# The FFN tail of a gated expert block: who rounds to the fp8 grid, TensorE or VectorE

## The chip, the core and the metric

The kernel runs on one core of one Trainium2 chip. The metric is the time of one execution on the device in microseconds (us). Names: PE is TensorE (matrix multiply), DVE is VectorE, ACT is ScalarE, POOL is GpSimd, SP is SyncE.

## The reference

The input is 2048 tokens of 512 values. A first part (layer norm, then one of four expert MLPs chosen by the token's id, added back with a gate) is the same before and after. The tail is what matters here:

```python
def _quant_e4m3(t):
    amax = jnp.max(jnp.abs(t)).astype(jnp.float32)
    scale = jnp.maximum(amax / E4M3_MAX, 1e-12)
    fp8 = (t.astype(jnp.float32) / scale).astype(jnp.float8_e4m3fn)
    return (fp8, scale)
...
w_fp8, w_scale = _quant_e4m3(weight)
x_fp8, x_scale = _quant_e4m3(x2d)
out2d = _scaled_mm(x_fp8, w_fp8.T, x_scale, w_scale)   # fp32 product * (sa*sb), then bf16
...
x = x + jnp.tanh(g_ffn[0]) * _L0_ffn_ref(_layernorm(x, axis=-1), L0_ffn_weight)
```

The scale is the maximum over the whole tensor, so nothing of the tail can start before the last token's second layer norm is known. Every value is then rounded to the e4m3 grid (three mantissa bits), multiplied by a 512x512 rounded weight and added to the residual.

## The kernel before

The tokens are sorted by expert into 16 tiles of 128 (a tile is 128 partitions x 512 values). The residual `x1` and the normalised rows `h2` of all tiles lie in SBUF. After the maximum is known (about 153 us into the span) the tail runs over 10 groups of tiles, set by `FIRST` (L168): group 0 is tile 0, group 1 tile 1, groups 2 to 7 are two tiles each (2-3, 4-5, 6-7, 8-9, 10-11, 12-13), group 8 is tile 14 and group 9 tile 15.

Rounding works without an fp8 type. A magic number `vm` is made from the value's size, the scaled value is added to it (`vt`, fp32), and subtracting `vm` again leaves the value rounded to the grid. The subtraction can be done in two places:

- on DVE: `rounded` (L1086) writes `q8 = vt - vm` in bf16, and PE transposes `q8` by multiplying it with the identity (L584, four bf16 products a tile);
- on PE: the transpose itself does it. `vm` is multiplied with the negative identity (L575, four bf16 products) and `vt` with the fp32 identity (L578, four fp32 products) into the same PSUM, so the sum that stands there is `vt - vm`, transposed.

`split(g)` (L259) says which tiles of a group go which way, by `BY_TENSOR` (L170). With 2, the groups 0 to 2 (tiles 0 to 3) are rounded by PE alone. In every later group the first tile is rounded by DVE and, where there is a second one, that one by PE. These are seven tiles on DVE: 4, 6, 8, 10, 12, 14 and 15.

Each engine has its own fixed order, and semaphores join them:

- ACT, in group g's turn: copy the transposed group out of PSUM (`copy_qT`, L727), the scaled absolute value of group g+4 (`scaled`, L721), and the product of group g-1 out of PSUM as bf16 (`to_bf16`, L736, "y" below).
- DVE, in group g's turn: `grid(g+1)` (L1073), `shifted(g)` (L1079), `rounded(g)` (L1086), and `finish(g-3)` (L1090), which adds the gated product to the residual.
- PE: `transposed(g+1)` (L575, L578, L584), then the four products a tile of group g with the rounded weight (L599, "the final products" below). Then the next group.
- POOL: sixteen stores in the order of the tiles (`store_tile`, L365). Each is an indirect DMA that puts a tile's rows back in the tokens' order, and waits until its group is finished.

So a group's way is: transposed, copied, multiplied, "y", finished, stored. Below, store n is the store of tile n.

Of the kernel before, what the change touches and what calls it, by code (L numbers as in the profile page):

```python
# [43 lines left out]
def gated_experts_kernel(nc, x, ids, ctx_t, g_x, g_f, wf_t, out):  # L44
# [10 lines left out]
    with ExitStack() as stack:  # L55
        def sb(name, shape, dt):
            return stack.enter_context(nc.sbuf_tensor(name, shape, dt))
# [109 lines left out]
        qT = sb("qT", [P, NF, D], BF16)  # L167
        FIRST = [0, 1, 2, 4, 6, 8, 10, 12, 14, 15, TILES]  # L168
        GROUPS = len(FIRST) - 1
        BY_TENSOR = 2  # L170
        y8 = sb("y8", [P, NB, D], BF16)

        four_ps = psum("four_ps", [P, 4 * D], F32)
# [82 lines left out]
        def tiles_of(g):  # L256
            return range(FIRST[g], FIRST[g + 1])

        def split(g):  # L259

            tiles = list(tiles_of(g))
            return (tiles[:1], tiles[1:]) if g > BY_TENSOR else ([], tiles)

# [155 lines left out]
        def _(pe):  # L419
# [147 lines left out]
            def transposed(g):  # L567
# [12 lines left out]
                if by_dve:  # L580
                    pe.wait_ge(q8_done, g - BY_TENSOR)
                for i in by_dve:
# [551 lines left out]
```

## Time and profile before

| | before |
|---|---|
| median of 3 runs | 196.71 us (196.63 to 196.82) |
| profiled execution, its own time | 196.66 us |
| its span (first to last instruction) | 194.8 us |
| PE / DVE / ACT / POOL busy, share of the span | 80% / 77% / 57% / 43% |
| start of the last store in the span | 189.05 us |

The tail is the last fifth of the span. Shares over the whole span say little about it, so the rows below are cut by time: start in us from the span's beginning, then duration in us. A row with "x8" stands for eight instructions in a row. The ends of PE's rows are modelled, so where PE runs without a gap, what a piece of work occupies is read from one row's start to the next row's start. Each fp32 product shows as two matmul records.

### The profile page before, as it was taken

What the parts mean: (1) busy time and instruction counts of PE and PEld (TensorE: products, weight loads), DVE (VectorE), ACT (ScalarE), POOL (GpSimd) and SP (SyncE); (2) the same over time, 40 slices, a digit from 0 to 9 for tenths busy, and PEclk for the clock granted to TensorE, in tenths of its full rate; (3) what the DMA queues carried; (4) which work ended last, traced back from release to release, by engine and by line L of the source; (5) the groups of instructions that cost most, each with busy time, mean ns of one, the idle gap of its engine ahead of it and who ended that gap; (6) DMA issues with size and microseconds to landing.
All of it is one profiled execution on the core that took longest, in us unless ns stands there. A gap on an engine that the chain in (4) does not pass through costs nothing.

```text
span 194.8 us, 3253 instructions
## 1 busy us (share of the span) xinstructions
PE 156.2 (80%) x822; PEld 80.3 (41%) x828; DVE 151.0 (77%) x346; ACT 112.0 (57%) x166; POOL 83.0 (43%) x117
## 2 busy tenths in 40 slices
PE   0151969799999799899999899999978799999300
PEld 0110435244555344444444445545433487765000
DVE  2876799898766799899998888677686698999600
ACT  3256698597342855767797644334322698977500
POOL 8258887512311443224456685111102003588770
PEclk9999999999999999999999999999999999999955
DMA  0937998400000221122211211000000001133351
GB/s 3 359 125 191 377 400 273 113 2 0 0 3 0 56 54 30 27 54 57 54 29 40 44 27 27 3 0 0 2 5 0 0 0 57 54 162 162 162 217 54
DMA packets 15440, 15.68 MB, mean 80 GB/s; under 512 B 10816, under 2 KB 11328, under 8 KB 15424
## 3 DMA queue, kind: packets, MB, share of 16 engines
q1 hardware_dynamic: 12576, 7.09, 12.1%
q0 software_dynamic: 2560, 8.39, 12.0%
q8 instruction: 8, 0.13, 0.3%
q14 instruction: 8, 0.07, 0.1%
q10 hardware_dynamic: 288, 0.00, 0.1%
HBM read 8.92 MB, written 4.19 MB: 67 GB/s over the span
## 4 chain that ended last, share of the span: by engine, by line
PE 35%; DVE 29%; issue 14%; POOL 12%; ACT 5%; DMA 1%; DVEq 1%; POOLq 0%
PE four_ps L466 9%; PE four_ps L458 9%; PE four_ps L475 9%; POOL out L365 6%; POOL x L342 3%; DVE zT_lo L899 3%; PE four_ps L504 3%; DVE bn L865 3%; DVE bn L913 2%; DVE w_lo L857 2%; PE q_ps L578 2%; DVE x L907 2%; DVE z L894 1%; DMA ids_s<-in_ids 1%; POOL rstd L352 1%
## 5 line engine op out<-in xcount | busy, mean ns | idle before, releaser
L360 POOL TENSOR_TENSOR rstd<-var,minus_half 128x1 f32<-128x1 f32 x16 | 8.8, 550 | 49.8 <-DVE var L921 49.8
L365 POOL DMA_INDIRECT out<-x,token_of x16 | 20.1, 1255 | 19.9 <-DVE x L1090 15.9
L458 PE MATMUL four_ps<-w_hi,hT_hi 128*128 x76 | 21.4, 393 | 1.4 <-ACT w_hi L626 1.3
L665 ACT ACTIVATE zT_hi<-four_ps 128x512 f16<-128x512 f32 x19 | 11.3, 595 | 18.2 <-PE four_ps L504 18.2
L654 ACT ACTIVATE sg<-four_ps,job_inv_a 128x512 f32<-128x512 f32 x19 | 12.9, 679 | 13.7 <-PE four_ps L475 12.5
L342 POOL DMA_INDIRECT x<-in_x,token_of x16 | 17.4, 1091 | 7.1 <-issue 4.2
L458 PE MATMUL four_ps<-w_hi,zT_hi 128*128 x76 | 19.5, 379 | 1.1 <-DVE x L907 1.1
L645 ACT ACTIVATE w<-x,nmr,rstd 128x512 f32<-128x512 f32 x16 | 13.0, 810 | 12.8 <-DVE nmr L927 12.4
L466 PE MATMUL four_ps<-w_lo,hT_hi 128*128 x76 | 19.7, 381 | 0.0
L475 PE MATMUL four_ps<-w_hi,zT_lo 128*128 x76 | 19.5, 379 | 0.0
L466 PE MATMUL four_ps<-w_lo,zT_hi 128*128 x76 | 19.5, 379 | 0.0
L907 DVE SCALAR_TENSOR_TENSOR x<-four_ps,job_mul,x 128x512 f32 x19 | 14.2, 746 | 6.2 <-PE four_ps L475 6.1
L504 PE MATMUL four_ps<-ident,z 128*128 128x128 f32 x76 | 12.1, 281 | 5.2 <-DVE z L894 4.9
L599 PE MATMUL four_ps<-wf_q,qT 128*128 128x512 bf16 x60 | 15.1, 379 | 0.8 <-ACT qT L727 0.6
L475 PE MATMUL four_ps<-w_hi,hT_lo 128*128 x60 | 15.4, 379 | 0.0
L640 ACT ACTIVATE h<-x,nmr,rstd 128x512 f32<-128x512 f32 x16 | 12.9, 804 | 3.5 <-DVE nmr L881 3.5
L894 DVE SCALAR_TENSOR_TENSOR z<-four_ps,job_z_mul,sg 128x512 f32<-128x512 f32 x16 | 12.0, 749 | 3.4 <-ACT sg L654 3.4
L352 POOL TENSOR_TENSOR rstd<-var,minus_half 128x1 f32<-128x1 f32 x16 | 8.9, 556 | 12.7 <-DVE var L873 12.6
L899 DVE TENSOR_TENSOR zT_lo<-four_ps,zT_hi 128x512 f16<-128x512 f32 x19 | 13.1, 690 | 0.6
L626 ACT ACTIVATE w_hi<-w,w_bits 128x512 f16<-128x512 f32 x16 | 10.2, 711 | 5.8 <-DVE w_bits L810 5.8
L504 PEld LDWEIGHTS four_ps<-ident,z 128*128 128x128 f32 x76 | 8.5, 140 | 11.7 <-DVE z L894 9.1
L857 DVE SCALAR_TENSOR_TENSOR w_lo<-w,w_bits,w_hi 128x512 f16<-128x512 f32 x16 | 11.6, 750 | 1.8 <-ACT w_hi L626 1.7
(146 smaller groups left out, 316.7 us busy)
## 6 DMA issues: line engine op xcount, KB each, us to landing
w<-in_ctx_t SPq DMA_DIRECT2D x4, 1024.0 KB, 9.4
wf<-in_wf_t SPq DMA_DIRECT2D x1, 512.0 KB, 15.1
x<-in_x,token_of POOLq DMA_INDIRECT x16, 5.7
out<-x,token_of POOLq DMA_INDIRECT x16, 2.9
hT_hi<-h_row SPq DMA_TRANSPOSE x9, 2.3
hT_lo<-h_row SPq DMA_TRANSPOSE x9, 2.3
ids_s<-in_ids SPq DMA_DIRECT2D x1, 8.0 KB, 2.9
g_s<-in_g_x ACTq DMA_DIRECT2D x1, 0.5 KB, 2.7
```

The lines of the kernel that those rows point to most:

```text
L342: pool.indirect_dma_start(block_of(x1, i), None, x, bass.IndirectOffsetOnAxis(ap=token_of[:, i:i + 1], axis=0), bounds_check=T - 1).then_i ...
L365: pool.indirect_dma_start(out, bass.IndirectOffsetOnAxis(ap=token_of[:, i:i + 1], axis=0), block_of(x1, i), None, bounds_check=T - 1).then ...
L458: pe.matmul(ps, lhs_hi(k), w_block(w_hi, expert, k), start=(k == 0), stop=False)
L466: mm = pe.matmul(ps, lhs_hi(k), w_block(w_lo, expert, k), start=False, stop=(first is not None and k == K - 1))
L475: mm = pe.matmul(ps, lhs_lo(k), w_block(w_hi, expert, k), start=False, stop=(k == K - 1))
L504: mm = pe.transpose(zT_ps[:, k * P:(k + 1) * P], z[:, k * P:(k + 1) * P], ident[:, :])
L599: mm = pe.matmul(four_ps[:, i % 4 * D:(i % 4 + 1) * D], qT[:, i % NF, k * P:(k + 1) * P], wf_q[:, k * D:(k + 1) * D], start=(k == 0), stop ...
L645: act.activation(block_of(h2, i), block_of(x1, i), ACT.Identity, bias=nmr2[:, :], scale=rstd2[:, :])\
L857: dve.scalar_tensor_tensor(out=w_block(w_lo, e, k), in0=w_block(w32, e, k), scalar=w_scale(e, S_W), in1=w_block(w_hi, e, k), op0=ALU.mult, ...
L894: dve.scalar_tensor_tensor(out=z[:, :], in0=a_ps[:, :], scalar=job_z_mul[:, j:j + 1], in1=sg[:, :], op0=ALU.mult, op1=ALU.mult).then_inc(z ...
L899: dve.tensor_tensor(zT_lo[:, :], zT_ps[:, :], zT_hi[:, :], ALU.subtract).then_inc(zT_lo_done, 1)
L907: dve.scalar_tensor_tensor(out=block_of(x1, tile), in0=y_ps[:, :], scalar=job_mul[:, bass.ds(j, 1)], in1=block_of(x1, tile), op0=ALU.mult, ...
```

## The change

`BY_TENSOR` becomes `GROUPS`, which is 10. No group's number is larger than that, so `split` gives every tile to PE.

```diff
-        BY_TENSOR = 2
+        BY_TENSOR = GROUPS
```

The function that reads it, and what PE does with the answer (the lines are the same before and after):

```python
def split(g):
    tiles = list(tiles_of(g))
    return (tiles[:1], tiles[1:]) if g > BY_TENSOR else ([], tiles)
...
for i in by_pe:      # vm with minus_ident (bf16), vt with ident (fp32)
...
if by_dve:           # q8 with ident_bf
    pe.wait_ge(q8_done, g - BY_TENSOR)
```

On PE, the order of the program in groups 3 to 9 (of each group of two tiles, `q_ps` is the PSUM that takes the transposed tiles, `hT_hi` holds `vm` and `q8`, `w_hi` holds `vt`, `four_ps` takes the final products):

```order
 L575 MATMUL q_ps<-minus_ident,hT_hi 128x128 x4
 L578 MATMUL q_ps<-ident,w_hi 128x128 x4
-L584 MATMUL q_ps<-ident_bf,hT_hi 128x128 x4
+L575 MATMUL q_ps<-minus_ident,hT_hi 128x128 x4
+L578 MATMUL q_ps<-ident,w_hi 128x128 x4
 L599 MATMUL four_ps<-wf_q,qT 128x512 x8
```

In the place of the four bf16 products of the DVE-rounded tile stand four bf16 and four fp32 products. Groups 8 and 9, of one tile each, change in the same way.

On DVE, the turns of groups 5 and 6:

```order
 L1073 TENSOR_SCALAR hT_hi<-hT_lo 128x1024
 L1079 SCALAR_TENSOR_TENSOR w_hi<-w,x_inv,hT_hi 128x1024
-L1086 TENSOR_TENSOR hT_hi<-w_hi,hT_hi 128x512
 L1090 SCALAR_TENSOR_TENSOR x<-y,tg,x 128x1024
 L1073 TENSOR_SCALAR hT_hi<-hT_lo 128x1024
 L1079 SCALAR_TENSOR_TENSOR w_hi<-w,x_inv,hT_hi 128x1024
-L1086 TENSOR_TENSOR hT_hi<-w_hi,hT_hi 128x512
 L1090 SCALAR_TENSOR_TENSOR x<-y,tg,x 128x1024
```

The rounding between `shifted` and `finish` is gone, in all seven groups; nothing else moves on DVE. ACT, POOL and SP have the same instructions in the same order.

## Rows read from the trace of the kernel before

**Rows 1.** Chain of waits, merged, in the tail: start, us, engine, tile, line

```profile
166.44 0.69 DVE hT_hi L1086
167.13 1.24 DVE x L1090
...
169.16 1.57 POOL out L365
```

**Rows 2.** Stretches: busy us of each engine, granted TensorE clock, DMA share, GB/s

```profile
158.90:161.25 2.35, 2.35 (x25) 2.32 (x24) 2.30 (x4) 1.56 (x2) 0.00 (x0) 1.00 0.00 0
162.10:177.90 15.80, 15.64 (x122) 11.00 (x124) 15.01 (x20) 13.48 (x15) 10.40 (x8) 1.00 0.24 100
182.60:190.00 7.40, 0.00 (x0) 0.00 (x0) 1.11 (x2) 0.68 (x1) 5.88 (x6) 0.73 0.44 180
```

**Rows 3.** Timeline of PE: start us, us, line, operation, count, [idle before <-releaser]

```profile
160.08 0.39 PE L575 MATMUL q_ps<-minus_ident,hT_hi 128*128 128x128 bf16 x4
160.30 1.11 PE L578 MATMUL q_ps<-ident,w_hi 128*128 128x128 f32 x8
161.25 1.03 PE L599 MATMUL four_ps<-wf_q,qT 128*128 128x512 bf16 x4
...
163.28 0.39 PE L584 MATMUL q_ps<-ident_bf,hT_hi 128*128 128x128 bf16 x4
163.51 1.89 PE L599 MATMUL four_ps<-wf_q,qT 128*128 128x512 bf16 x7
165.23 0.39 PE L575 MATMUL q_ps<-minus_ident,hT_hi 128*128 128x128 bf16 x4
...
175.99 1.89 PE L599 MATMUL four_ps<-wf_q,qT 128*128 128x512 bf16 x7
...
177.94 1.89 PE L599 MATMUL four_ps<-wf_q,qT 128*128 128x512 bf16 x8
...
179.89 1.03 PE L599 MATMUL four_ps<-wf_q,qT 128*128 128x512 bf16 x4
181.52 1.04 PE L599 MATMUL four_ps<-wf_q,qT 128*128 128x512 bf16 x4 [0.61 <-ACT qT L727]
```

**Rows 4.** Timeline of POOL: the stores

```profile
171.04 1.62 POOL L365 DMA_INDIRECT out<-x,token_of  x1 [0.30 <-issue]
...
177.88 0.97 POOL L365 DMA_INDIRECT out<-x,token_of  x1 [0.30 <-issue]
...
183.45 1.47 POOL L365 DMA_INDIRECT out<-x,token_of  x1 [0.30 <-issue]
185.22 0.97 POOL L365 DMA_INDIRECT out<-x,token_of  x1 [0.30 <-issue]
...
189.05 0.97 POOL L365 DMA_INDIRECT out<-x,token_of  x1 [0.30 <-issue]
```

**Rows 5.** Groups of DVE's instructions, 158 to 185 us: busy us, mean ns

```profile
L1086 DVE TENSOR_TENSOR hT_hi<-w_hi,hT_hi 128x512 bf16<-128x512 f32 x7 | 4.8, 692 | 0.2
```

**Rows 6.** Timeline of DVE

```profile
170.53 1.28 DVE L1090 SCALAR_TENSOR_TENSOR x<-y,tg,x 128x1024 f32<-128x1024 bf16 x1
...
177.84 0.75 DVE L1079 SCALAR_TENSOR_TENSOR w_hi<-w,x_inv,hT_hi 128x512 f32<-128x512 f32 x1
...
181.01 1.95 DVE L1090 SCALAR_TENSOR_TENSOR x<-y,tg,x 128x1024 f32<-128x1024 bf16 x2 [0.49 <-ACT y L736]
183.31 0.75 DVE L1090 SCALAR_TENSOR_TENSOR x<-y,tg,x 128x512 f32<-128x512 bf16 x1 [0.36 <-ACT y L736]
```

**Rows 7.** Timeline of ACT, the last groups

```profile
179.87 1.11 ACT L736 ACTIVATE y<-four_ps,out_scale 128x1024 bf16<-128x1024 f32 x1 [0.35 <-PE four_ps L599]
180.88 0.59 ACT L727 ACTIVATE qT<-q_ps 128x512 bf16<-128x512 f32 x1
...
182.60 0.69 ACT L736 ACTIVATE y<-four_ps,out_scale 128x512 bf16<-128x512 f32 x1 [0.55 <-PE four_ps L599]
```

## Prediction, made before the changed kernel ran

> **What bounds the kernel now.** I read the chain of waits first, then busy time by stretch, then the timeline of one engine after the other in the tail. Three things can be seen.
>
> The chain [rows 1] runs through DVE's rounding (166.44), the finish of group 2 behind it (end 168.37) and then into POOL's stores, which stand on it from 169.16 to the end. So from there the stores set the end: 0.79 us from the end of a finish to its store, and then store after store. Where DVE is idle a store takes 0.97 and the next follows after 0.30, so 1.27 each (the last four starts in [rows 4]). Where a DVE instruction is already running as a store starts, the store is longer: store 3 at 171.04 started under a finish that ran from 170.53 to 171.81 [rows 6] and took 1.62; store 11 at 183.45 started under one that ran to 184.06 and took 1.47. A store that starts no later than about the DVE instruction isn't held: store 7 at 177.88 beside 177.84, 0.97. So a held store takes what is left of the DVE instruction (0.77 and 0.61), plus 0.85.
>
> The chain hides how close PE is to being the bound. From 162.10 to 177.90 PE is busy 15.64 of 15.80 us at a granted clock of 1.00, more than DVE with 15.01 [rows 2]. After 182.6 PE does nothing and POOL works through a backlog. How big the backlog is: group 7's finish is the first of the two at 181.01, so with 1.28 it ends at 182.29, and store 12 could start at 183.08. It starts at 185.22 [rows 4, 6]. PE's way to the end thus has 2.14 us in hand at tile 12, no more.
>
> **The change part by part.**
>
> *Removed from DVE:* seven roundings of 0.69, 4.8 us [rows 5]. They matter where finishes wait for DVE, as in rows 1. I cost this at nothing in the sum, because a finish also needs its product, and PE delivers that later (next step). With the roundings gone, DVE is no engine that anything waits for.
>
> *Added on PE:* seven tiles go by L575 and L578 in the place of L584. What such a tile occupies can be read in this trace, since group 2 has one: 160.08 to 161.25, 1.17 us from start to start. A tile by L584 occupies 163.28 to 163.51, 0.23 [rows 3]. So 0.94 more a tile. Bounds for it: if the four bf16 products with the negative identity cost nothing (they start at 160.08 and the fp32 ones at 160.30, so 0.22), 0.72; if the modelled row lengths are right instead of the starts, 0.39 + 1.11 - 0.39 = 1.11. I take 0.94, since the starts of neighbouring rows show it in full.
>
> PE has no gap to put this in, so it adds up. The final products of group g stand behind the transposes of group g+1, so those of group 6 come five tiles late, of group 7 six, of group 8 seven. A group of two tiles takes 1.17 + 1.17 + 1.72 = 4.06 (the 1.72 is 163.51 to 165.23) in the place of 3.12. Two stores take at most 2 x 1.93 (171.04's 1.62 + 0.30, doubled) = 3.84, less than 4.06: POOL has no backlog any more, and each group's first store waits for PE. ACT's copy, scaled value and "y" of a group are about 3.3 and fit too.
>
> *The end, step by step.* Group 6: final products at 175.99 + 5 x 0.94 = 180.69, end + 1.89 = 182.58. "y" follows after 0.04 (182.56 to 182.60 before) with 1.11: 183.73 [rows 7]. Finish after 0.02 with 1.28: 185.03. Store 10 after 0.79: 185.82, DVE idle; store 11 at 187.09.
> Group 7: products at 177.94 + 6 x 0.94 = 183.58, end 185.47, "y" to 186.62, finish 186.64 to 187.92. Store 11 starts under this finish with 0.83 of it left: 0.85 + 0.83 = 1.68, end 188.77. Store 12 would be ready at 187.92 + 0.79 = 188.71 and starts 0.30 after store 11: 189.07.
> Group 8: products at 179.89 + 7 x 0.94 = 186.47, end (1.03) 187.50, "y" (0.69) 188.23, finish (0.75) to 189.00.
> Group 9: it waited 0.61 before, for ACT's copy, which stood behind group 7's "y" [rows 3, 7]. Now that "y" ends at 186.62 and the copy (0.59) at about 187.25, while PE is in group 8's products until 186.47 + 0.86 = 187.33. So that wait goes. Products to 188.37, "y" to 189.10, finish to 189.87, store 15 ready at 190.66.
> Stores 12, 13, 14, 15: 189.07, 190.34, 191.61, 192.88, all clear of DVE or only just. The last store was at 189.05, so **+3.83**. What follows the last store is the same. 196.66 + 3.83 = 200.49 for the profiled execution, and the median lies 0.05 above that execution: **200.5 us**.
>
> If store 12 comes just after the last finish has started (189.12) instead of just before, it is held by 0.63: 201.2. With 0.72 a tile, six tiles in front of group 7 take off 6 x 0.22 = 1.32: 199.2. With 1.11 they add 6 x 0.17 = 1.02, and with the held store 202.2.
>
> The Trainium skill's "SBUF — State Buffer", section "Who interferes with whom", has a rule that bears on the stores: a VectorE instruction with two SBUF inputs and a GpSimd instruction that reads SBUF exclude each other, and whichever comes second waits for all of the other. The two held stores and the free one above agree with it. L1086 has two SBUF inputs, so by the rule the change would take away up to 4.8 us in which a store can be held, which is an argument for rival 1; it does not touch the sum, where POOL waits for PE.
>
> **The rivals.**
>
> 1. *Faster: the stores stay the bound.* If the longer transposes cost PE little, nothing but the freed DVE is left: finishes come earlier, fewer stores are held. From the same first store of the backlog (169.16), thirteen steps of 1.27 end at 185.67 in the place of 189.05: 196.66 - 3.38 = 193.3 us at best. It decides at the slack of tile 12: 2.14 us over six tiles, 0.36 a tile. Below that the end is POOL's as before or better, above it PE's. For it: the chain names DVE and POOL there and not PE, and the ends of PE's rows are modelled. Against it: starts are not modelled, and group 2 shows 0.94.
> 2. *No difference:* the added tile costs about 0.36 and the slack eats it: 196.7 us. For and against as in 1; it needs an even closer hit.
> 3. *Slower by much: PE's clock falls.* PE would spend a larger part of its time on passes against an identity. If that lowered the granted clock from 1.00 (2.4 GHz) to the lower level of 1.2 GHz, the stretch from 162.1 to the end of my group 9 at 188.4, some 26 us, would take twice as long: about 227 us. The trace speaks against it: from 158.90 to 161.25 PE does nothing but one group's transposes (the end of one final product aside) and keeps 1.00; the mean of 0.73 comes only after 182.6, when PE has stopped [rows 2]. The Trainium skill's "TensorE: Matmul & The Clock Gate", section "Part 4: PE-mode transpose", says that transposes in the transpose mode do not count as activity for the clock; L575 and L578 are ordinary products with an identity, and no run here shows the other kind in such a stretch.
>
> **How the numbers follow.** My forecast, 199.2 to 202.2 with 200.5 in it, has 0.89. Slower, but by less than 199.2, because something on the way gives back more than I see: 0.04. Rival 3: 0.01. Rival 2: 0.02. Rival 1: 0.04. A measurement of this kernel can tell 0.2% (0.4 us) from no change. So faster 0.04, same 0.02, slower 0.94. The range 199.0 to 202.2 is the forecast's own bounds with a little below.
>
> **What would show it.** In the profile after, PE should stand without a gap until about 188.4, a group of two tiles every 4.06 us, and each tile in groups 3 to 9 should occupy 1.17 in the transposes. The waits of POOL should be for DVE's finish at each group's first store, and DVE should have idle time that ends with ACT's "y". The last store should start near 192.9. The forecast is wrong if the fp32 products of a DVE-rounded tile take less than they do in group 2, if PE's final products get faster beside them, or if the stores still run without waiting from 169 us on.

## The result, and the profile after

The changed kernel takes **200.44 us** (200.43 to 200.56, 4 runs), the kernel before beside it 196.76. The ratio is 1.0189, 95% interval 1.0176 to 1.0201: slower by 1.9%, where 200.5 us was forecast.

| | before | after |
|---|---|---|
| profiled execution, its time / span | 196.66 / 194.8 us | 200.56 / 198.8 us |
| PE / DVE busy, share of the span | 80% / 77% | 82% / 74% |
| start of the last store | 189.05 us | 193.04 us |

The timeline of PE after, to be laid beside [rows 3]:

```profile
163.37 0.39 PE L575 MATMUL q_ps<-minus_ident,hT_hi 128*128 128x128 bf16 x4
163.59 1.11 PE L578 MATMUL q_ps<-ident,w_hi 128*128 128x128 f32 x8
164.53 1.89 PE L599 MATMUL four_ps<-wf_q,qT 128*128 128x512 bf16 x8
166.26 0.39 PE L575 MATMUL q_ps<-minus_ident,hT_hi 128*128 128x128 bf16 x4
...
168.60 1.89 PE L599 MATMUL four_ps<-wf_q,qT 128*128 128x512 bf16 x8
...
180.80 1.89 PE L599 MATMUL four_ps<-wf_q,qT 128*128 128x512 bf16 x8
...
183.70 1.89 PE L599 MATMUL four_ps<-wf_q,qT 128*128 128x512 bf16 x8
...
186.59 1.89 PE L599 MATMUL four_ps<-wf_q,qT 128*128 128x512 bf16 x8
```

Where the four products of group 3 by L584 stood before (163.28 to 163.51 in [rows 3]), a second L575 and L578 now occupy 163.37 to 164.53, 1.16 us. The final products of one group start 4.07 us after those of the last (164.53, 168.60). Groups 8 and 9 run into each other at 186.59: the wait of 0.61 for the copy is gone. In the stretch that [rows 2] show (columns as there), PE's gap is closed and DVE is now a good deal less busy:

```profile
162.10:177.90 15.80, 15.80 (x128) 12.19 (x126) 10.69 (x13) 11.60 (x13) 8.91 (x7) 1.00 0.25 100
```

The timeline of POOL after, beside [rows 4], and of DVE's last finishes, beside [rows 6]:

```profile
169.92 1.58 POOL L365 DMA_INDIRECT out<-x,token_of  x1 [2.56 <-DVE x L1090]
171.80 2.00 POOL L365 DMA_INDIRECT out<-x,token_of  x1 [0.30 <-issue]
...
177.83 0.97 POOL L365 DMA_INDIRECT out<-x,token_of  x1 [1.35 <-DVE x L1090]
179.10 0.97 POOL L365 DMA_INDIRECT out<-x,token_of  x1 [0.30 <-issue]
181.90 0.97 POOL L365 DMA_INDIRECT out<-x,token_of  x1 [1.83 <-DVE x L1090]
183.17 0.97 POOL L365 DMA_INDIRECT out<-x,token_of  x1 [0.30 <-issue]
185.96 0.97 POOL L365 DMA_INDIRECT out<-x,token_of  x1 [1.82 <-DVE x L1090]
187.24 1.67 POOL L365 DMA_INDIRECT out<-x,token_of  x1 [0.31 <-issue]
189.21 0.98 POOL L365 DMA_INDIRECT out<-x,token_of  x1 [0.30 <-DVE x L1090]
...
193.04 0.97 POOL L365 DMA_INDIRECT out<-x,token_of  x1 [0.30 <-issue]
```

```profile
183.88 1.28 DVE L1090 SCALAR_TENSOR_TENSOR x<-y,tg,x 128x1024 f32<-128x1024 bf16 x1 [2.12 <-ACT y L736]
186.77 1.28 DVE L1090 SCALAR_TENSOR_TENSOR x<-y,tg,x 128x1024 f32<-128x1024 bf16 x1 [1.61 <-ACT y L736]
188.38 1.62 DVE L1090 SCALAR_TENSOR_TENSOR x<-y,tg,x 128x512 f32<-128x512 bf16 x2 [0.32 <-ACT y L736]
```

And ACT's "y" of group 6, ahead of the finish at 183.88:

```profile
182.73 1.11 ACT L736 ACTIVATE y<-four_ps,out_scale 128x1024 bf16<-128x1024 f32 x1 [0.70 <-PE four_ps L599]
```

Before, the stores stood back to back from 169.16 on. Now the first stores of groups 4, 5 and 6 (177.83, 181.90, 185.96) wait 1.35 to 1.83 us for a finish, the finishes wait for ACT's "y", and that waits for PE. Store 11 at 187.24 is held by the finish at 186.77.

**A ledger.** From store 2 to store 15 there are thirteen steps of 1.27, together 16.51. What else lies between them is "held", the time that stores took over 0.97 (summed over stores 2 to 15), and "waiting", the time that POOL stood idle over 0.30 (summed). The start of store 2, plus 16.51, plus these two, is the start of the last store. Waiting is given as what is left in that sum; the rounded rows bear it out to 0.1 us, so values under 0.1 mean none. Medians are of fast runs beside the kernel before, which had 196.7 to 196.8 each time. v1 to v3 are the versions at the end of the experiments.

| kernel | store 2 starts | held | waiting | last store | median |
|---|---|---|---|---|---|
| before | 169.16 | 3.30 | 0.08 | 189.05 | 196.7 |
| after | 169.92 | 2.47 | 4.14 | 193.04 | 200.44 |
| e1, PE's part alone | 169.83 | 2.95 | 3.65 | 192.94 | 200.40 |
| e2, DVE's part alone | 169.32 | 3.32 | 0.07 | 189.21 | 196.77 |
| e3, cheap second pass | 169.13 | 4.64 | 0.08 | 190.36 | 197.83 |
| e4, two early tiles | 170.04 | 4.54 | 0.07 | 191.16 | 198.57 |
| e8, three early tiles | 169.90 | 4.44 | 1.10 | 191.95 | 199.52 |
| e6, two late tiles | 169.19 | 3.77 | 0.06 | 189.53 | 197.04 |
| e5, finish from PSUM | 169.07 | 2.39 | 0.07 | 188.04 | 195.83 |
| e7, e5's finish in the changed kernel | 169.77 | 1.77 | 4.48 | 192.53 | 200.05 |
| v1 / v2 / v3 | 169.21 / 169.21 / 169.50 | 2.81 / 2.40 / 2.41 | 0.07 / 0.08 / 0.06 | 188.60 / 188.20 / 188.47 | 196.29 / 195.76 / 195.86 |

After against before: 0.76 later start, 0.83 less held, 4.06 more waiting, 3.99 together. Where nothing ahead of store 2 was changed, its start still differs by up to 0.43 (169.07 in e5, 169.50 in v3). Store 0 differs by as much already (162.03, 162.45), so the reasons lie ahead of the tail.

### The profile page after: what moved, and what is told of

Its sections match the earlier page's. It is cut to its first block, busy times and chain, and to the rows that moved or that the text cites. A ratio compares the mean times of both kernels' runs of the same rounds, so it can differ in the third digit from the quotient of the medians.

```text
span 198.8 us, 3364 instructions
## 1 busy us (share of the span) xinstructions
PE 162.5 (82%) x884; PEld 86.7 (44%) x884; DVE 146.7 (74%) x339; ACT 112.6 (57%) x166; POOL 82.2 (41%) x117
## 3 DMA queue, kind: packets, MB, share of 16 engines
HBM read 8.92 MB, written 4.19 MB: 66 GB/s over the span
## 4 chain that ended last, share of the span: by engine, by line
PE 45%; DVE 27%; issue 10%; POOL 9%; ACT 4%; DMA 1%; DVEq 1%; POOLq 0%
PE four_ps L466 9%; PE four_ps L458 9%; PE four_ps L475 9%; PE q_ps L578 7%; PE four_ps L599 5%; POOL x L342 3%; POOL out L365 3%; DVE zT_lo L899 3%; PE four_ps L504 3%; DVE bn L865 3%; DVE bn L913 2%; DVE w_lo L857 2%; PE q_ps L575 2%; DVE x L907 2%; DVE z L894 1%
## 5 line engine op out<-in xcount | busy, mean ns | idle before, releaser
L365 POOL DMA_INDIRECT out<-x,token_of x16 | 19.2, 1203 | 24.6 <-DVE x L1090 21.9
L1090 DVE SCALAR_TENSOR_TENSOR x<-y,tg,x 128x1024 f32<-128x1024 bf16 (+1 forms) x10 | 10.7, 1071 | 11.9 <-ACT y L736 11.8
L578 PE MATMUL q_ps<-ident,w_hi 128*128 128x128 f32 x128 | 17.8, 282 | 0.0
L578 PEld LDWEIGHTS q_ps<-ident,w_hi 128*128 128x128 f32 x128 | 15.6, 192 | 0.0
```

Of the source, the lines that this page charges most:

```text
L365: pool.indirect_dma_start(out, bass.IndirectOffsetOnAxis(ap=token_of[:, i:i + 1], axis=0), block_of(x1, i), None, bounds_check=T - 1).then ...
L578: mm = pe.matmul(q_block(i, k), vt[:, i % NB, k * P:(k + 1) * P], ident[:, :], start=False, stop=(k == K - 1))
```

## The experiments

**e1: PE's part of the change alone**, with the changed kernel as the base. DVE rounds the seven tiles still, for nobody.

```diff
-                i = split(g)[0][0]
+                i = FIRST[g]
...
-                    if split(g)[0]:
+                    if g > 2:
                         rounded(g)
```

> TensorE transposes and rounds every tile, as in the changed kernel, and VectorE still does its seven roundings, whose results nobody reads: the change's TensorE part alone. My theory (TensorE's 0.94 us a tile is the whole cost, the freed VectorE time is worth nothing behind it): within 0.7 us of the changed kernel, 200.4 to 201.1 us, the surplus only where a rounding holds a store. Rival (the change lost more on TensorE than it shows, and the 4.8 us freed on VectorE pays a good part of it back): 202 to 205 us.

Measured: 200.40 us, ratio 1.0189 (1.0176 to 1.0202), the changed kernel's own. With PE slower, putting the seven roundings back costs nothing, so taking them out had brought nothing there.

**e2: DVE's part alone**, with the kernel before as the base.

```diff
-                if by_dve:
-                    pe.wait_ge(q8_done, g - BY_TENSOR)
...
-                        mm = pe.matmul(q_block(i, k), q8[:, i % NB, k * P:(k + 1) * P], ident_bf[:, :],
+                        mm = pe.matmul(q_block(i, k), vm[:, i % NB, k * P:(k + 1) * P], ident_bf[:, :],
...
-                    if split(g)[0]:
-                        rounded(g)
```

> VectorE rounds nothing, and TensorE does what it did before in time: for the seven tiles it transposes the bf16 magic numbers in the place of the rounded values (left out: those tiles' values themselves). The change's VectorE part alone. My theory: TensorE's final products keep their starts (175.99 us for group 6), stores are held less, last store near 187.5 us in place of 189.05, time about 195.1 us, between 193.3 (nothing ever held, rival 1 of the prediction) and 196.4. Rival (VectorE was no bound either, the stores are on their own): 196.7 us, no difference.

Measured: 196.77 us, ratio 1.0002 (0.9994 to 1.0011). My theory's 195.1 was wrong. The stores of e2, one `grid` (L1071 in e2) and its last finishes:

```profile
171.21 1.09 POOL L365 DMA_INDIRECT out<-x,token_of  x1 [0.30 <-issue]
...
176.69 1.54 POOL L365 DMA_INDIRECT out<-x,token_of  x1 [0.30 <-issue]
178.54 0.97 POOL L365 DMA_INDIRECT out<-x,token_of  x1 [0.30 <-issue]
179.82 1.54 POOL L365 DMA_INDIRECT out<-x,token_of  x1 [0.30 <-issue]
181.66 1.64 POOL L365 DMA_INDIRECT out<-x,token_of  x1 [0.30 <-issue]
183.61 1.47 POOL L365 DMA_INDIRECT out<-x,token_of  x1 [0.31 <-issue]
...
189.21 0.97 POOL L365 DMA_INDIRECT out<-x,token_of  x1 [0.30 <-issue]
```

```profile
171.16 0.28 DVE L1071 TENSOR_SCALAR hT_hi<-hT_lo 128x512 bf16<-128x512 bf16 x1
...
179.22 1.28 DVE L1088 SCALAR_TENSOR_TENSOR x<-y,tg,x 128x1024 f32<-128x1024 bf16 x1 [1.18 <-ACT y L734]
181.17 1.95 DVE L1088 SCALAR_TENSOR_TENSOR x<-y,tg,x 128x1024 f32<-128x1024 bf16 x2 [0.66 <-ACT y L734]
183.48 0.75 DVE L1088 SCALAR_TENSOR_TENSOR x<-y,tg,x 128x512 f32<-128x512 bf16 x1 [0.36 <-ACT y L734]
```

Stores 3 to 6 are held less and run ahead. Then store 7 starts under a finish that runs from 176.10, and stores 9, 10 and 11 under those at 179.22, 181.17 and 183.48, and all four are held. The sum held is what it was before, 3.32 and 3.30. The rival's time was right, but not its reason: the stores are not on their own. Finishes, which come when PE and ACT let them, catch the stores again.

**e3: a cheap second pass**, e2 with four more bf16 products for each of the seven tiles.

```diff
+                    for k in range(K):
+                        pe.matmul(q_block(i, k), vm[:, i % NB, k * P:(k + 1) * P], minus_ident[:, :],
+                                  start=(k == 0), stop=False)
```

> VectorE rounds nothing, and TensorE takes two bf16 passes (magic number with the negative identity, then with the identity) for the seven tiles: 0.22 us a tile in the place of 0.94 (left out: those tiles' values). My theory, with the break-even of 0.36 us a tile: faster than before or equal, 195.3 to 196.7 us, and TensorE's final products of group 7 start 1.3 us later than before. Rival (any extra TensorE time is paid in full from the first tile on, the slack is not there): 1.3 us above the kernel with the VectorE part alone. Second rival (the second pass costs as much as an fp32 one): about 200 us.

Measured: 197.83 us, ratio 1.0058 (1.0045 to 1.0071), 1.06 above e2. On PE the extra pass costs what it should:

```profile
163.25 0.39 PE L582 MATMUL q_ps<-minus_ident,hT_hi 128*128 128x128 bf16 x4
163.48 0.39 PE L585 MATMUL q_ps<-ident_bf,hT_hi 128*128 128x128 bf16 x4
163.70 1.89 PE L600 MATMUL four_ps<-wf_q,qT 128*128 128x512 bf16 x8
```

So 0.22 a tile, below my break-even of 0.36, still makes the kernel slower. My theory fell, and the first rival (1.3) was nearly right.

**e4, e8 and e6: fewer tiles, early and late.** The base is the kernel before. The comments in the cut are not in the code.

```diff
-        BY_TENSOR = 2
+        BY_TENSOR = 4        # e4; e8 has 5
...
-            return (tiles[:1], tiles[1:]) if g > BY_TENSOR else ([], tiles)
+            return (tiles[:1], tiles[1:]) if BY_TENSOR < g < 8 else ([], tiles)   # e6, BY_TENSOR = 2
```

> BY_TENSOR = 4: only tiles 4 and 6 (groups 3 and 4) go over to TensorE, five tiles stay on VectorE. Simple slack theory, as in the prediction: 2 x 0.94 = 1.88 us is less than the 2.14 us that tile 12 had in hand, so no difference, 196.5 to 197.0 us. Rival (the slack at tile 12 is not the measure: the stores of the backlog start when group 2 is finished, and that comes 0.7 us later as in the changed kernel, with other stores held by VectorE): 197.4 to 198.3 us.

> BY_TENSOR = 5: tiles 4, 6 and 8 go over to TensorE. Theory A (0.94 us a tile in full from the first on): 196.7 + 2.82 = 199.5 us. Theory of the prediction (2.14 us in hand at tile 12): 0.7 us slower than before, 197.4 us. In between, 198.6 to 199.2 us: stores start 0.7 us later at tile 2, and held stores make the rest.

> Two tiles go over to TensorE as in e4, but the two last ones (14 and 15, groups 8 and 9) in the place of tiles 4 and 6. Theory A (every extra 0.94 us of TensorE is paid in full, less the 0.61 us that TensorE waited for the last group): 1.88 - 0.61 = 1.27 us slower, 198.0 us. Theory H (what counts is when the stores start and which finishes catch them; late in the tail the backlog of stores covers TensorE): 196.0 to 197.2 us, no difference within 0.5.

Measured: e4 198.57 us (1.0094, 1.0080 to 1.0109), e8 199.52 (1.0150, 1.0131 to 1.0170), e6 197.04 (1.0012, 1.0003 to 1.0021). Two early tiles cost 1.88 against the kernel before beside them, three 2.76: 0.94 and 0.92 a tile, paid in full. That is more than both theories of e4 gave; theory A of e8 had its time. Two late ones cost 0.3, as theory H of e6 had it. All seven cost 3.7, so the four that e8 leaves on DVE cost 0.9 together.

The reason can be read from the end of the last finish (group 9). It is at 184.06 before, 184.23 in e2, 185.38 in e3, 186.17 in e4 and 186.97 in e8, and the last store starts 4.98 or 4.99 after it in all five. There group 9's finish catches store 11, so the stores behind it are counted from that finish, and its time is PE's (and ACT's) time. In e4:

```profile
185.42 0.75 DVE L1090 SCALAR_TENSOR_TENSOR x<-y,tg,x 128x512 f32<-128x512 bf16 x1 [0.36 <-ACT y L736]
```

```profile
185.55 1.47 POOL L365 DMA_INDIRECT out<-x,token_of  x1 [0.30 <-issue]
...
191.16 0.97 POOL L365 DMA_INDIRECT out<-x,token_of  x1 [0.30 <-issue]
```

Stores 9 and 10 of e4 (181.86, 183.60) start under finishes too (from 181.16 and 183.11) and take 1.43 and 1.65, so these stores move with PE.

In e6 it comes at 185.21, 1.15 later than before, but the last two finishes run from 183.60 and the second begins at about 184.46, just after store 11:

```profile
183.60 1.61 DVE L1090 SCALAR_TENSOR_TENSOR x<-y,tg,x 128x512 f32<-128x512 bf16 x2 [0.32 <-ACT y L736]
```

```profile
184.43 0.97 POOL L365 DMA_INDIRECT out<-x,token_of  x1 [0.30 <-DVE x L1090]
...
189.53 0.97 POOL L365 DMA_INDIRECT out<-x,token_of  x1 [0.30 <-issue]
```

Store 11 is not held there, and the last store comes only 0.48 later. In the changed kernel the last finish ends at 190.00 and the last store starts 3.04 after it, for the same reason: store 12 at 189.21 starts just ahead of that finish (about 189.25) and is free.

**e5 and e7: a finish that holds no store.** The finishes of groups 7 to 9 read the product from PSUM; base of e5 is the kernel before, of e7 the changed one.

```diff
-                dve.scalar_tensor_tensor(out=rows_of(x1, g), in0=ring(y8, g, NB), scalar=tg[:, 1:2],
+                product = ring(four_ps[:, :].rearrange("p (b d) -> p b d", d=D), g, 4)
+                dve.scalar_tensor_tensor(out=rows_of(x1, g), in0=product if g >= 7 else ring(y8, g, NB), scalar=tg[:, 1:2],
```

> The kernel before, but the finishes of groups 7 to 9 read the product from PSUM in the place of its bf16 copy in SBUF, after the same wait (left out for these four tiles: the output scale and the rounding to bf16). Such a finish has one SBUF input instead of two. Theory H (a store that starts under a VectorE instruction with two SBUF inputs is held until it ends): stores 10 and 11 take 0.97 in the place of 1.39 and 1.47, last store 0.92 us earlier, 195.8 us. Rival (those stores are longer for another reason, as the transfers beside them): no difference, 196.7 us.

> The changed kernel with the edit of e5 (the same parts left out). Theory H: only store 11 (1.67 us) is held by these finishes; it takes 0.97, but store 12 must then wait for group 7's finish, so the last store comes 0.4 us earlier, 200.1 us. If the end were set by held stores alone: 0.7 us or more, 199.7 us or less. Rival (no holding): 200.4 us.

Measured: e5 195.83 us (0.9952, 0.9938 to 0.9965), e7 200.05 (1.0168, 1.0154 to 1.0182). Both are theory H's numbers. e5's finishes stand where they stood and take as long. Store 10 at 181.65 starts under one and is short; store 11 at 182.93 now comes ahead of the last finish:

```profile
180.92 1.94 DVE L1091 SCALAR_TENSOR_TENSOR x<-four_ps,tg,x 128x1024 f32<-128x1024 f32 x2 [0.49 <-ACT y L736]
183.23 0.75 DVE L1091 SCALAR_TENSOR_TENSOR x<-four_ps,tg,x 128x512 f32<-128x512 f32 x1 [0.36 <-ACT y L736]
```

```profile
181.65 0.97 POOL L365 DMA_INDIRECT out<-x,token_of  x1 [0.30 <-issue]
182.93 0.97 POOL L365 DMA_INDIRECT out<-x,token_of  x1 [0.30 <-DVE x L1091]
...
188.04 0.97 POOL L365 DMA_INDIRECT out<-x,token_of  x1 [0.30 <-issue]
```

This shows that a finish holds a store only with both of its inputs in SBUF. The same is seen in e7, whose store 11 at 187.09 takes 0.97 in the place of 1.67 in the changed kernel, and below with the other input moved. The Trainium skill, "SBUF — State Buffer", section "Who interferes with whom", says that a VectorE instruction with at most one SBUF input does not contend with GpSimd outside the modes that use two ports; e5's store at 181.65 under such a finish, 0.97 in the place of 1.39, agrees.

**v1 to v3: a version that beats both.** What e5 found can be had with every rounding in place: ScalarE copies the residual of a group into a part of PSUM that has already been copied out, and the finish takes it from there. The comments in the cut are not in the code.

```diff
+            def x_to_psum(first, n, copied):
+                act.wait_ge(qT_copied, copied)
+                out = q_ps[:, first % 4 * D:(first % 4 + n) * D]
+                act.activation(out, x1[:, first * D:(first + n) * D], ACT.Copy).then_inc(x_copied, 1)
...
+                if g == 7:                       # v2; v3 copies tile 12 here and tile 13 in the next turn, v1 tile 15 at the end
+                    x_to_psum(12, 2, 8)
...
+                residual = rows_of(x1, g)
+                if g == 7:                       # v1: 9
+                    dve.wait_ge(x_copied, 1)
+                    residual = ring(q_ps[:, :].rearrange("p (b d) -> p b d", d=D), g, 4)
...
-                                         in1=rows_of(x1, g), op0=ALU.mult, op1=ALU.add).then_inc(out_done, 1)
+                                         in1=residual, op0=ALU.mult, op1=ALU.add).then_inc(out_done, 1)
```

> The kernel before, with the residual of the last tile copied by ScalarE into PSUM (a copied-out part of q_ps), so that group 9's finish reads one input from SBUF and one from PSUM. Everything is computed as before. Theory H: store 11 is not held by that finish, 0.97 in the place of 1.47, 0.5 us faster than before, 196.2 us. Rival (the copy delays ScalarE's last product and the end with it): no gain or up to 0.6 us slower.

> The same for group 7 (two tiles, one copy of 1024 columns after the group is copied out). Everything is computed as before. Theory H: store 10 is not held, store 11 then starts before group 9's finish and is not held either: 0.42 + 0.50 = 0.92 us faster, 195.8 us, as in e5. Rival: the copy takes 1.1 us in a gap of 0.7 us of ScalarE, so group 6's and 7's finishes come 0.4 us later and catch other stores, which gives back up to 0.5 us: 196.3 us.

> As v2, the two tiles copied one by one, each into a gap of ScalarE (0.70 and 0.35 us). Everything is computed as before. Theory H: between 195.8 and 196.1 us; group 7's finish comes 0.25 us later, so that group 8's can catch store 11. Rival (holding is decided by the copies' place on ScalarE): like before, 196.7 us.

Measured: v1 196.29 us (0.9975, 0.9961 to 0.9989), v2 195.76 (0.9942, 0.9921 to 0.9963), v3 195.86 (0.9946, 0.9927 to 0.9964). v2 and v3 can't be told apart. All three are faster than the kernel before, and v2 by 4.7 us than the changed one. v2's copy on ACT, its last finishes and its stores:

```profile
177.29 1.03 ACT L744 ACTIVATE q_ps<-x 128x1024 f32<-128x1024 f32 x1
178.25 1.10 ACT L737 ACTIVATE y<-four_ps,out_scale 128x1024 bf16<-128x1024 f32 x1
179.24 0.59 ACT L728 ACTIVATE qT<-q_ps 128x512 bf16<-128x512 f32 x1
```

```profile
181.06 1.28 DVE L1103 SCALAR_TENSOR_TENSOR x<-y,tg,q_ps 128x1024 f32<-128x1024 bf16 x1 [0.39 <-ACT y L737]
...
183.36 0.75 DVE L1103 SCALAR_TENSOR_TENSOR x<-y,tg,x 128x512 f32<-128x512 bf16 x1 [0.36 <-ACT y L737]
```

```profile
181.81 0.97 POOL L366 DMA_INDIRECT out<-x,token_of  x1 [0.30 <-issue]
183.09 0.97 POOL L366 DMA_INDIRECT out<-x,token_of  x1 [0.31 <-DVE x L1103]
...
188.20 0.97 POOL L366 DMA_INDIRECT out<-x,token_of  x1 [0.30 <-issue]
```

Store 10 at 181.81 is free under the finish from 181.06, so store 11 starts at 183.09, ahead of the last finish (183.36), and is free too. The copy fills ACT's gap there and moves group 6's "y" by 0.3; of the later stores only store 9 pays for it, with 0.02 (0.99 in the place of 0.97). v1's store 11 at 183.49 and v3's store 10 at 182.08 start under such finishes as well and take 0.97.

## Why the prediction was right, point by point

- *Added on PE, 0.94 a tile:* right. 1.16 for such a tile and 4.07 a group were measured (1.17 and 4.06 in the working). e4 and e8 show the same price in the time, e1 that it is all of the change's cost.
- *Removed from DVE, nothing in the sum:* right, and more so than I thought. e1 and e2 both find nothing, with PE slow and with PE as before.
- *The end, step by step:* right. Final products at 180.80, 183.70 and 186.59 (worked out 180.69, 183.58, 186.47); store 10 at 185.96 (185.82); store 11 held for 1.67 (1.68); store 12 at 189.21 (189.07); last store at 193.04 (192.88). Half of the difference is a tail that started 0.08 later. That the time fits to 0.1 us has some luck in it: store 12 was to start 0.05 ahead of the last finish and started about 0.04 ahead, a margin finer than the working can promise. The prediction gave 201.2 for the other order.
- *POOL without a backlog:* right for groups 4 to 6. The "at most 3.84" for two stores was too low: store 3 at 171.80 was held for 2.00, longer than the 1.62 that the working took, so stores 2 and 3 took 4.19 (169.92 to 174.11) and group 3's first store still came without a wait. The end does not rest on it.
- *PE's clock, rival 3:* the granted clock is 1.00 throughout the stretch with more identity passes in it, from 162.10 to 188.50.
- *The slack of 2.14 us, and the break-even of 0.36 a tile, which decided rivals 1 and 2:* wrong. e3, with 0.22 a tile, was to be no slower and is 1.1 us slower; e4, with 1.88 in all, was to make no difference and costs 1.88. I took POOL's backlog as free time that PE could use. It was not free: a store of the backlog is held by the finish that runs as it starts, a later PE makes that finish later, and the hold then ends later by as much. The forecast did not rest on this step, because it went store by store through the changed kernel's own end, holds included. Rival 1's price had the same flaw: 193.3 took every hold away, and e2 shows that freeing DVE takes none away in sum.

## What to carry to other kernels

A queue with a backlog is not slack, as long as the engine that feeds it can also block it: work out the start of each element with its holds, and do not subtract two ends. When an engine is freed and nothing comes of it, look whether the waits that it caused have moved rather than gone; the sum of held time (3.30 and 3.32 here) shows it in one number. And before work is moved to the engine that looks less busy over the whole span, read the busy time in the stretch where it is to go: PE was at 15.64 of 15.80 us there.

## What the runs showed of the hardware that I had not expected

- The prediction's "what is left of the DVE instruction, plus 0.85" fits the held stores from store 2 on, in all thirteen traces, to within 0.01 us.
- Holding goes one way in these traces. A store that starts under a DVE instruction with two SBUF inputs is held, while a finish that starts just after a store is not lengthened: v2's finish at 183.36, beside store 11 from 183.09, took its usual 0.75, and so did e6's from about 184.46 beside store 11 from 184.43. The prediction said that the traces agree with a rule by which whichever comes second waits. For the store that is so, for the DVE instruction it is not.
- Less than a tenth of a microsecond decides it. The store at 177.88 before [rows 4] started 0.04 after L1079 at 177.84 [rows 6], and neither was held (0.97 and 0.75). e1's store 8 at 181.81 started 0.10 after a rounding at 181.71 and took 1.44.
- A second SBUF input is not the only thing that holds a store. e2's store 3 at 171.21 took 1.09 while a `grid` with one SBUF input was running from 171.16: 0.24 left, plus 0.85. Why it holds, no run shows.
- One input in PSUM instead of SBUF changed nothing in the finish's own length (0.75 for 512 columns, 1.28 for 1024) and ended the holding.
- What in the two-SBUF-input instruction holds the store (its reads or something else) stays open; no run tells it apart.
